# Layer 2 cross attention: the sums of squared queries by one-column products instead of turned queries

## What is computed

```python
def rmsnorm(x, g, eps=EPS):
    var = jnp.mean(jnp.square(x), axis=-1, keepdims=True)
    return x * jax.lax.rsqrt(var + eps) * g
q = rmsnorm((hidden_states @ Wq).reshape(B, Sq, H, D), gq)
k = rmsnorm((encoder_hidden_states @ Wk).reshape(B, Skv, H, D), gk)
scores = jnp.einsum('bqhd,bkhd->bhqk', q, k) * (1.0 / np.sqrt(D))
out = jnp.einsum('bhqk,bkhd->bqhd', softmax(scores), v)
```

## Time and profile before

| what | value |
|---|---|
| median of 3 runs | 2254.61 us (2248.16 to 2255.44) |
| the profiled execution's own time | 2253.01 us |
| its span | 2251.2 us |
| mean granted TensorE clock, as a share of 2.4 GHz | 0.847 |
| busy share of TensorE, its weight loads, VectorE, ScalarE, GpSimd | 80%, 58%, 62%, 37%, 15% |
| the changed block: first key rows to last projection | 947.6 to 1299.6 us |
| queries turned on TensorE (L1740) | 128 transposes, 20.9 us busy |
| their squares on ScalarE (L1989) | 128 with 128 accumulator reads, 33.6 and 26.5 us busy |
| the roots on GpSimd (L2074, L2076) | 32 and 32, 6.4 and 32.6 us busy |

### The profile page before, as it was taken

One profiled execution on the slowest core, in us unless ns is written; L12 is line 12 of the kernel. 1 busy time (PEld: TensorE's weight loads), 2 busy tenths in 40 slices (PEclk: granted clock), 3 DMA queues, 4 the chain that ended last, 5 costly groups with the idle time before them and its releaser, 6 DMA issues.

```text
span 2251.2 us, 31833 instructions
## 1 busy us (share of the span) xinstructions
PE 1809.7 (80%) x12358; PEld 1314.9 (58%) x12358; DVE 1406.2 (62%) x2536; ACT 828.8 (37%) x1955; POOL 330.3 (15%) x313
## 2 busy tenths in 40 slices
PE   8767697647636777679999879997999989999795
PEld 4444444314413445557777758886888767777552
DVE  7579848679888551545655549995555634555315
ACT  2745303265322016366666521112444424344100
POOL 2335400015401014121212100000000000000100
PEclk9965587655566989899999989998999989999766
DMA  4010110100010220120000020001002030000100
GB/s 127 2 39 0 16 48 5 59 0 1 1 47 1 41 78 2 32 100 1 1 1 1 1 80 1 1 1 47 11 10 66 1 94 1 1 1 1 38 0 19
DMA packets 29087, 55.11 MB, mean 24 GB/s; under 512 B 6742, under 2 KB 22131, under 8 KB 27388
## 3 DMA queue, kind: packets, MB, share of 16 engines
q1 hardware_dynamic: 28940, 53.10, 7.9%
HBM read 45.35 MB, written 1.05 MB: 21 GB/s over the span
## 4 chain that ended last, share of the span: by engine, by line
PE 51%; DVE 16%; issue 4%; ACT 3%; POOL 2%; DMA 1%; SPq 1%; DVEq 0%; POOLq 0%; ACTq 0%
PE banks L1783 8%; PE banks L1766 7%; PE banks L1801 6%; PE banks L1695 6%; DVE big L966 3%; PE banks L2532 3%; PE banks L2545 3%; DVE big L558 2%; PE banks L2568 2%; PE banks L1723 2%; PE banks L466 1%; PE banks L477 1%; PE banks L2744 1%; PE banks L1740 1%; SPq L366 1%
## 5 line engine op out<-in xcount | busy, mean ns | idle before, releaser
L1876 DVE TENSOR_REDUCE arena<-banks 128x2 f32<-128x512 f32 x192 | 132.3, 689 | 351.8 <-PE banks L1766 351.8
L2004 ACT ACTIVATE big<-banks,arena 128x256 f32<-128x256 f32 x384 | 189.9, 502 | 119.3 <-DVE arena L1876 99.2
L1766 PE MATMUL banks<-big 128*128 128x256 f32 x768 | 206.8, 393 | 2.9 <-ACT big L2004 2.9
L220 POOL TENSOR_TENSOR ln_rstd<-ln_var_eps,neg_half 128x2 f32<-128x2 f32 x48 | 36.6, 762 | 1166.8 <-DVE ln_var_eps L200 1166.8
L1783 PE MATMUL banks<-big 32*128 32x256 f32 x3072 | 183.3, 386 | 11.2 <-DVE big L1894 10.0
L1801 PE MATMUL banks<-big 128*128 128x256 f32 x768 | 181.2, 381 | 0.3 <-ACT x_feat L244 0.3
L1695 PE MATMUL banks<-x_feat,arena 128*128 128x256 f32 x768 | 176.9, 384 | 0.0
L1783 PEld LDWEIGHTS banks<-big 32*128 32x128 f32 x3072 | 158.0, 188 | 31.1 <-DVE big L1894 12.4
L1766 PEld LDWEIGHTS banks<-big 128*128 128x128 f32 x768 | 137.5, 191 | 45.9 <-issue 32.5
L1801 PEld LDWEIGHTS banks<-big 128*128 128x128 f32 x768 | 144.7, 190 | 28.9 <-issue 9.4
L1695 PEld LDWEIGHTS banks<-x_feat,arena 128*128 128x128 f32 x768 | 148.6, 194 | 22.1 <-issue 1.3
(11 more groups left out here) (337 smaller groups left out, 3160.7 us busy)
## 6 DMA issues: line engine op xcount, KB each, us to landing
big<-big SPq DMA_DIRECT2D x128, 32.0 KB, 1.9
big<-in_ctx_tok SPq DMA_DIRECT2D x8, 512.0 KB, 7.9
big<-big SPq DMA_DIRECT2D x32, 64.0 KB, 2.3
arena<-in_L0f_w SPq DMA_DIRECT2D x1, 2048.0 KB, 8.1
arena<-in_L1a_wo SPq DMA_DIRECT2D x1, 2048.0 KB
arena<-in_L1f_gv SPq DMA_DIRECT2D x1, 2048.0 KB
arena<-in_L2a_qk_w SPq DMA_DIRECT2D x1, 2048.0 KB
arena<-in_L2x_q_w SPq DMA_DIRECT2D x1, 2048.0 KB
```

What stands on the lines that cost most here:

```text
L1766: last = mm(ps[:, h * SEQ:(h + 1) * SEQ], self.q[:, n % 2, r, h * P:(h + 1) * P], k, start=not self.mask, stop=True, skip_group_check=self ...
L1876: ins = v.tensor_reduce(dst, B[4 + u % 2][:].rearrange("p (h k) -> p h k", h=2), AX.X, ALU.max, negate=True)
L2004: last = a(self.probs[:, u % 3, h, :], B[4 + u % 2][:, h * SEQ:(h + 1) * SEQ], ACT.Exp, bias=self.neg_max[:, u % 4, h:h + 1], scale=scale, ...
```

## The change

A unit's queries are no longer turned. ScalarE squares all four heads of a unit in one instruction as they lie in SBUF (1024 elements a partition, `q_sq`, one buffer of the same size as the two before). TensorE multiplies each 128x128 tile of the squares, as weights, with one column of ones: eight products for a unit, each giving 128 sums over the channels in one column of bank 6. ScalarE copies the eight columns to SBUF and adds eps on the way (Identity with a bias from a pointer). GpSimd takes one power of eight columns instead of two additions and two powers of four.

The places: on ScalarE the square stands between the second eviction of queries and the evictions of turned keys, and the copy behind the outputs; on TensorE the products stand behind the values. Bank 6's order changes with it. VectorE waits once for a unit's roots instead of twice.

```diff
@@ count_places
             if self.each and ahead:
-                put("k_turn", n + 1, 0), put("k_turn", n + 1, 1), put("q_turn", n + 1, 0)
+                put("k_turn", n + 1, 0), put("k_turn", n + 1, 1), put("q_sums", n + 1)
...
-            if self.each and ahead:
-                put("q_turn", n + 1, 1)
@@ tensor
-        def turn_queries(n, half):
-            claim("q_turn", n, half)
-            pe.wait_ge(self.q_read, 2 * n + half + 1)
-            for r in range(2):
+        def sum_queries(n):
+            claim("q_sums", n)
+            pe.wait_ge(self.q_squared, n + 1)
+            for r in range(QUAD):
                 for t in range(2):
-                    last = turn(B[6][:, (2 * r + t) * P:(2 * r + t + 1) * P], self.q[:, n % 2, 2 * half + r, t * P:(t + 1) * P], e.ident[:])
+                    last = mm(B[6][:, 2 * r + t:2 * r + t + 1], self.q_sq[:, r, t * P:(t + 1) * P], e.ones[:, 0:1], start=True, stop=True)
             last.then_inc(self.misc_psum, 1)
...
-            turn_queries(0, 0), turn_queries(0, 1)
+            sum_queries(0)
...
             if 1 <= n <= self.n:
                 values(n - 1)
+            if self.each and ahead:
+                sum_queries(n + 1)
@@ scalar
+        def square_queries(n):
+            act.wait_ge(self.q_read, 2 * n + 2)
+            if n:
+                act.wait_ge(self.misc_psum, self.place["q_sums", n - 1] + 1)
+            a(self.q_sq, self.q[:, n % 2], ACT.Square).then_inc(self.q_squared, 1)
+
+        def sum_queries(n):
+            filled("q_sums", n)
             if n >= 2:
-                act.wait_ge(self.q_rooted, 2 * (n - 2) + half + 1)
...
+                act.wait_ge(self.q_rooted, n - 1)
+            a(self.q_ss[:, n % 2, :], B[6][:, 0:2 * QUAD], ACT.Identity, bias=self.eps[:, 0:1]).then_inc(self.misc_read, 1)
...
             if self.each and ahead:
+                square_queries(n + 1)
                 turn_keys(n + 1, 0), turn_keys(n + 1, 1)
-                turn_queries(n + 1, 0)
...
                 outputs(n - 1)
+            if self.each and ahead:
+                sum_queries(n + 1)
@@ gpsimd
-        def root_queries(n, half):
...
+        def root_queries(n):
+            pool.wait_ge(self.misc_read, self.place["q_sums", n] + 1)
             if n >= 2:
                 pool.wait_ge(self.exped, QUAD * (n - 1))
...
+            tt(self.q_rs[:, n % 2, :], self.q_ss[:, n % 2, :], e.neg_half[:, 0:2 * QUAD], ALU.pow).then_inc(self.q_rooted, 1)
```

More of the change, by code:

```diff
@@ L1573, in __init__ @@
             self.k_ss, self.k_rs = a.take(2 * QUAD), a.take(2 * QUAD)
-            self.k_tok, self.k_sq, self.q_sq = big.take(2, 2, QUAD * DH), big.take(2, QUAD * DH), big.take(2, QUAD, DH)
+            self.k_tok, self.k_sq, self.q_sq = big.take(2, 2, QUAD * DH), big.take(2, QUAD * DH), big.take(QUAD, SEQ)
         if mask:
@@ L1597, in __init__ @@
             self.k_rooted, self.k_normed = s(name + "_k_rooted"), s(name + "_k_normed")
-            self.q_squared, self.q_added, self.q_rooted = s(name + "_q_squared"), s(name + "_q_added"), s(name + "_q_rooted")
+            self.q_squared, self.q_rooted = s(name + "_q_squared"), s(name + "_q_rooted")
         if mask:
@@ L1617, in count_places @@
                 if n == 0:
-                    put("q_turn", 0, 0), put("q_turn", 0, 1)
+                    put("q_sums", 0)
             put("k_turn", 0, 0), put("k_turn", 0, 1)
@@ L1848, in tensor @@
                 project(n - 2, 0)
-            if self.each and ahead:
-                turn_queries(n + 1, 1)
             if live:
@@ L1879, in row_max @@
                 n, r = divmod(u, QUAD)
-                if r % 2 == 0:
-                    dve.wait_ge(self.q_rooted, 2 * n + r // 2 + 1)
+                if r == 0:
+                    dve.wait_ge(self.q_rooted, n + 1)
                 ins = v.tensor_tensor(self.neg_max[:, u % 4, :], self.raw_max[:, u % 4, :], self.q_rs[:, n % 2, 2 * r:2 * r + 2], ALU.mult)
@@ L1979, in turn_keys @@
             a(self.k[:, n % 3, 2 * half:2 * half + 2, :].rearrange("p h t -> p (h t)"), B[6][:], ACT.Copy, scale=self.gain).then_inc(self.misc_read, 1)
-        def turn_queries(n, half):
-            filled("q_turn", n, half)
-            if n >= 2:
-                act.wait_ge(self.q_rooted, 2 * (n - 2) + half + 1)
[L1985 to L1990, removed]
+        def square_queries(n):
[5 more added lines that the diff above has]
+            filled("q_sums", n)
+            if n >= 2:
+                act.wait_ge(self.q_rooted, n - 1)
+            a(self.q_ss[:, n % 2, :], B[6][:, 0:2 * QUAD], ACT.Identity, bias=self.eps[:, 0:1]).then_inc(self.misc_read, 1)
         def fold(g, half):
@@ L2022, in scalar @@
         if self.each:
-            turn_queries(0, 0), turn_queries(0, 1)
+            square_queries(0), sum_queries(0)
             key_rows(1, 0), key_rows(1, 1)
@@ L2067, in root_keys @@
             tt(self.k_rs, self.k_ss, e.neg_half[:, 0:2 * QUAD], ALU.pow).then_inc(self.k_rooted, 1)
-        def root_queries(n, half):
-            cols = slice(QUAD * half, QUAD * half + QUAD)
-            pool.wait_ge(self.misc_read, self.place["q_turn", n, half] + 1)
+        def root_queries(n):
+            pool.wait_ge(self.misc_read, self.place["q_sums", n] + 1)
             if n >= 2:
                 pool.wait_ge(self.exped, QUAD * (n - 1))
-            tt(self.q_ss[:, n % 2, cols], self.q_ss[:, n % 2, cols], self.eps[:, cols], ALU.add).then_inc(self.q_added, 1)
-            pool.wait_ge(self.q_added, 2 * n + half + 1)
-            tt(self.q_rs[:, n % 2, cols], self.q_ss[:, n % 2, cols], e.neg_half[:, 0:QUAD], ALU.pow).then_inc(self.q_rooted, 1)
+            tt(self.q_rs[:, n % 2, :], self.q_ss[:, n % 2, :], e.neg_half[:, 0:2 * QUAD], ALU.pow).then_inc(self.q_rooted, 1)
         if self.each:
             root_keys(0)
-            root_queries(0, 0), root_queries(0, 1)
+            root_queries(0)
             root_keys(1)
@@ L2085, in gpsimd @@
             if self.each and n + 1 < self.n:
-                root_queries(n + 1, 0)
-            if self.each and n + 1 < self.n:
-                root_queries(n + 1, 1)
+                root_queries(n + 1)
             if self.each and n + 2 < self.n:
```

## The result

| what | before | after |
|---|---|---|
| median of 7 runs each | 2254.61 us (2248.16 to 2255.44) | 2264.28 us (2259.77 to 2269.71) |
| ratio | | 1.0047, 95% interval 1.0031 to 1.0063 |
| profiled execution, mean granted clock | 2253.01 us, 0.847 | 2269.71 us, 0.842 |
| first key rows to the last values of the block | 341.0 us | 355.0 us |

The account below looks back on a forecast made before the run. TensorE, carrying 51% of the chain of waits, was taken as the bound, with ScalarE counting only where TensorE waits. Terms over units and start summed to -7.9 us: 2253.0 to 2245.1, named as 2246; range 2239 to 2258.

Parts of the forecast that it names:

- (a): On TensorE, plain units: the first half of the turned queries goes, so the values follow the keys sooner; gain 1.44 us.
- (b): On ScalarE: the square, 1.06 us, goes ahead of the key evictions; loss 0.17 us, or 1.09 where nothing hides it.
- (d): On TensorE, before the fourth score: the second half of the turned queries goes; gain 0.69 us.
- (e): GpSimd's four instructions a unit become one and ScalarE sheds squares and accumulator reads; costed at nothing.
- A to V: TensorE's stretch from a unit's first turn of keys to the start of its values; 3.42 us before, 2.15 forecast.
- S to A: TensorE's stretch from a unit's fourth score to the next first turn of keys; forecast unchanged at 7.86 us.
- V1: The first values in layer 2's cross attention; from the first key rows to them the forecast change was -1.95 us.
- (c): Behind the values: eight products at 0.112 us each, covered by ScalarE's output eviction; key rows held for the copy, loss 1.44.
- the hold: TensorE's key rows, sharing bank 6, wait until ScalarE has copied the sums; forecast loss 1.44 us a unit.
- a plain unit: A pass of the loop without layer norm, units 5, 7, 8, 9, 11, 12, 13; forecast 19.6 us instead of 20.13.
- a rule against it: On TensorE's products: the Trainium skill's four passes for a true FP32 product would make eight products four times dearer.
- rival 3: Slower: dear products between values and key rows; at 0.22 us each the sum is about +2, past 0.27 over +6.8; chance 0.08.

## Why the prediction was wrong

Right: (a), (b), (d) and (e), to 0.1 us each. A to V is 2.16, S to A 7.85, the copy and the square cost what was named, no unit lost its cover on GpSimd (a slip of 0.03 in the square's end, 1139.92 and not 1139.89, does not enter the sum), and with bf16 products the stretches behind V1 are the forecast ones to 0.1 us each, but for 0.3 in the last.

**The step that failed is (c),** by its count. "32 in 3.73 us" took the rows of the last layer's products for 32 products; they are 16 products of two instructions each, as one can see beforehand in the scores, two products in the code and x4 in the row. So 0.112 is the price of half an fp32 product. Eight cost 1.95, the hold is 2.30 instead of 1.44, a plain unit gains -1.44 + 0.17 + 2.30 - 0.69 = +0.34 (measured +0.35). The 12.3 of the units from V1 to V15 and the estimated 1.7 of the start and unit 0 turn -7.9 into about +6.

With it fell the passage "a rule against it". The row was said not to bear the rule out; it could not speak against it, since its spacing was that of the halves of products. The place and the kind of rival 3 were right, and at its row for 0.22 it gave +2; it had 0.08.

**The second failure is the clock,** which the prediction let move the start by a microsecond or two. The square ahead of the key evictions made TensorE wait 2.33 in pass 0 where it had waited 1.24, and the longer products with their hold were followed by falls in passes 1 and 4. In the profiled block the falls cost some 7.9 us, by the estimate above, the products having lengthened that of the start as well. The prediction named a clock leaving 1.00 inside 1014 to 1290 as a sign of being wrong, but range and chances took the 1.00 as given, only because it was so before.

Open: why the fall comes in pass 4 and not in 2 or 3, and why it moves when an earlier pass is filled. Also, the block is 14 us longer in both profiled executions, while the medians differ by 9.7 and 11.6. Outside the block the two took 2.8 us more and 0.6 us less than the execution before, so the rest of the kernel gave next to nothing back; whether the executions without a profile, from 2259.77 us at a clock of 0.848 up, have all of the falls is open.

## What to carry to other kernels

Divide a row's count by the products in the code before taking a duration from it: here an fp32 product was two instructions, and a sum over ones, of squares rounded to bf16, cost 0.35 us for what took 1.95 in fp32. Work put ahead of an instruction that shares its bank holds it until its own eviction has run, and that waits its turn on its engine: 2.30 us here in fp32, still 1.36 in bf16. So ask for the next place where the engine waits for another anyway, and whether that wait is as long as the work. Price a wait added early in a stage at both clocks.

## What the runs showed of the hardware

- Eight one-column fp32 products with weights of 128 columns are sixteen instructions and take 1.95 us; four with two columns are eight and take 1.05; sixteen with four columns are 32 and take 3.73. Between one and four columns the instructions count here, not the columns.
- The granted clock can fall while TensorE is busy by the rows: behind the 1.95 us of one-column products, from 1079.7 to 1083.2, with one idle time of 0.36 between, and none since the 1.05 us ahead of 1072.85. Behind 0.35 us of bf16 products, with a wait of 1.02 us after them, it stayed at 2.4 GHz.
- The falls repeat: two profiled executions of the changed kernel have them in the same passes, with the same stretches to 0.1 us.
